# First graph of a fused hypergraph and expert kernel: load order, magnitudes, degrees and order of work rewritten

## The chip, the cores and the metric

The kernel runs on one core of a Trainium2 chip. The metric is the device time of one execution in microseconds. Three executions of the kernel before took 727.12, 729.49 and 731.59 us (median 729.49).

## The reference

For each of 16 graphs, x is 512 x 256 and adj is 512 x 512:

```python
def hypergraph_conv(x, adj, W, b):
    H = (adj != 0); w = adj.reshape(N, -1)[:, :C]         # w is the first row of adj
    Dn = 1 / (H @ w)                                      # 0 where the sum is 0
    Be = 1 / H.sum(axis=1)                                # one over the degree of each hyperedge
    return Dn * (H @ (Be * (H.T @ (x @ W.T)))) + b
x = x + [ln -> conv(W1, b1) -> relu -> layer_norm(gamma, beta) -> conv(W2, b2), + its input]
x = x + [ln -> router, top 2 of 4 experts, silu, mask, out_w, + its input, rms norm]
```

## The kernel before, in words

Matmul operands are split into two float16 halves (hi and lo), so each product is two or three matmuls. A weight is first scaled by a power of two from its largest magnitude. The scale therefore needs, before any half is made: the weight loaded, the magnitude of each partition (`setup_abs_*` on ScalarE, `setup_mag_*` on VectorE), a transpose to one row (`turn_mags`), its maximum (`largest`), a matmul that spreads it over the partitions (`spread_max`), and a chain of small VectorE operations (`setup_scale_a`, `_b`, `_c` for W1, for gamma times W2 called w2g, and for the experts, out_w and the router). `setup_hi` on ScalarE and `setup_lo` on VectorE then make the halves.

`steps` calls `body` per graph on each engine. Step 0 holds only the convolution of graph 0 (`conv=True, ffn=False`) and the set-up. Step g from 1 holds the convolution of graph g and the expert layer of graph f = g - 1; a tail follows. Nothing plans the order: each engine works through its own list in program order and waits on semaphores.

One convolution on TensorE is: A1 = H.T x (`first` lines L1453, L1454), D (L1466, the product with w), A2 (`a2_half`, L1421), A3 with W1 (L1310 to L1312), transposes of the normed h (`transposed_h`), V with w2g (`v_tile`), U and B3 (`incidence`). ScalarE takes each result out of PSUM as hi (`a1_part`, `hnt_part`, `v_part`), VectorE as lo. GpSimd turns variances into scale and bias (`root`) and adds x, b2 and the bias row to `xb` by three accumulating DMAs (`add_x`, `add_b2`, `add_v`), each behind the one before. `x1_half` adds B3 to `xb`; from x1 come statistics, roots, `x2_part`, the turned x2, its halves `xth` and `xtl`, router and experts.

In step 0 the DMA queue of SyncE issues wrow, x, beta, gamma, W2, adj, W1, b1, adj transposed, then the six loads of the expert part. `first_ht` makes the transposed incidence in four pieces, each summing its degree; for all later graphs `count_edges` on ScalarE counts degrees. In step 0, PE opens with `beta_w2`. The magnitudes use a buffer `absbuf`, written by ScalarE and reduced by VectorE.

Of the kernel before, what the change touches and what calls it, by code (L numbers as in the profile page):

```python
# [47 lines left out]
def build(nc, x, adj, adjt, wrow, w1t, b1, gamma, beta, w2t, b2, rw, rb, ew, eb, ow, ob, nw, out):  # L48
# [7 lines left out]
    with ExitStack() as ctx:  # L56
# [3 lines left out]
        def sem(name):  # L60
# [4 lines left out]
        A1_BANK, D_BANK, A2_BANK = (0, 3), 2, (4, 1)  # L65
# [25 lines left out]
        absbuf = sb("absbuf", [P, 2, 1024], F32)  # L91
# [11 lines left out]
        ident16 = sb("ident16", [P, P], F16)  # L103
        epsln, epsrms = sb("epsln", [P, CT], F32), sb("epsrms", [P, CT], F32)
# [67 lines left out]
        table_set, a_abs, b_abs, c_abs, a_hi, b_hi, c_hi = (  # L172
            sem(n) for n in ("table_set", "a_abs", "b_abs", "c_abs", "a_hi", "b_hi", "c_hi"))
# [3 lines left out]
        a_lo, b_lo, c_lo = (sem(n) for n in ("a_lo", "b_lo", "c_lo"))  # L177
        bw_rdy, vb_set = sem("bw_rdy"), sem("vb_set")
# [62 lines left out]
        def _(sp):  # L241
            sp.dma_start(wf[:, :, :], wrow).then_inc(wrow_in, 16)
            sp.dma_start(xin[:, :, :], x[0]).then_inc(x_in, 16)
            for dst, src in ((bet[:, :], beta), (gam[:, :], gamma),
                             (w2f[:, :, :], w2t.rearrange("(k p) f -> p k f", p=P))):
                sp.dma_start(dst, src).then_inc(b_in, 16)
            sp.dma_start(adjin[:, :, :], adj[0].rearrange("(t p) e -> p t e", p=P)).then_inc(adj_in, 16)
            for dst, src in ((w1f[:, :, :], w1t.rearrange("(k p) h -> p k h", p=P)),
                             (b1b[:, :], b1.to_broadcast([P, DH]))):
                sp.dma_start(dst, src).then_inc(a_in, 16)  # L250
            sp.dma_start(adjtin[:, :, :], adjt[0].rearrange("(t p) c -> p t c", p=P)).then_inc(adjt_in, 16)
# [9 lines left out]
            def body(sp, g, odd, conv, ffn, late, prep):  # L261
# [14 lines left out]
                if prep:  # L276
                    sp.wait_ge(ht_made, g + 4)
# [19 lines left out]
        def _(gp):  # L297
# [13 lines left out]
            gp.wait_ge(tables, 12)  # L311
# [6 lines left out]
            for i, part in enumerate((0, NE)):  # L318
                gp.wait_ge(tables, 15 + i)
# [81 lines left out]
            prep_x(0, again=False)  # L401

            def body(gp, g, odd, conv, ffn, late, prep):
# [19 lines left out]
                if conv:  # L423
                    if not ffn:
                        add_x(g)
# [1262 lines left out]
```

## Time and profile before

| | |
|---|---|
| runs | 727.12, 729.49, 731.59 us |
| profiled execution | 727.4 us, span 725.9 us |
| mean granted TensorE clock | 0.989 |
| PE busy | 685.4 us, 94% |
| DVE busy | 622.8 us, 86% |
| ACT busy | 528.7 us, 73% |
| POOL busy | 342.7 us, 47% |
| chain that ended last | PE 87%, DVE 5%, ACT 3% |

PE is TensorE's matmuls, DVE is VectorE, ACT is ScalarE, POOL is GpSimd, SPq is SyncE's queue. Times are from the start of the span. The span is 1.5 us shorter than that execution's own time, which in turn is 2.1 us under the median of the runs.

### The profile page before, as it was taken

The numbers are of one execution on the slowest core, as the hardware profiler recorded it, in microseconds if no ns is written. First come the engines' busy times: TensorE is split into PE (matmuls) and PEld (weight loads), VectorE is DVE, ScalarE is ACT, GpSimd is POOL, SyncE is SP. The second block draws the span as 40 slices with busy tenths as digits, with TensorE's granted clock in tenths as the row PEclk, the third lists the DMA queues.
The fourth block names the chain that finished last, engine by engine and source line by source line (L and its number), as shares of the span: only waits on it lengthen the run. The fifth ranks groups of instructions, "written<-read, shape, count | busy, mean of one in ns | idle before, by whom it ended". The sixth has DMA issues, their size and how long they took to land.

```text
span 725.9 us, 15857 instructions
## 1 busy us (share of the span) xinstructions
PE 685.4 (94%) x5197; PEld 475.7 (66%) x5197; DVE 622.8 (86%) x1544; ACT 528.7 (73%) x1091; POOL 342.7 (47%) x731
## 2 busy tenths in 40 slices
PE   3777999999999999999999999999999999999982
PEld 2464485866758586775858577685857668585672
DVE  3987799898989989898989989898998989898676
ACT  4567868688696868778686877869686786967563
POOL 4142625456373545646354554635355563634433
PEclk9999999999999999999999999999999999999997
DMA  8547449575665938566583947657394756537312
GB/s 284 190 77 242 92 106 235 93 236 117 210 141 136 230 63 256 112 212 134 153 203 61 274 99 227 120 173 173 83 260 90 236 111 197 121 77 184 59 30 59
DMA packets 42591, 111.72 MB, mean 154 GB/s; under 512 B 4161, under 2 KB 5313, under 8 KB 42561
## 3 DMA queue, kind: packets, MB, share of 16 engines
q0 software_dynamic: 13536, 41.42, 32.8%
q1 hardware_dynamic: 29024, 69.92, 27.4%
q8 instruction: 16, 0.26, 0.1%
q14 instruction: 15, 0.11, 0.0%
HBM read 69.91 MB, written 16.25 MB: 119 GB/s over the span
## 4 chain that ended last, share of the span: by engine, by line
PE 87%; DVE 5%; ACT 3%; DMA 1%; issue 1%; POOL 1%; SPq 0%; POOLq 0%; DVEq 0%; ACTq 0%
PE bank L1310 16%; PE bank L1312 16%; PE bank L1311 16%; PE bank L1395 7%; PE bank L1396 7%; PE bank L1421 7%; PE bank L1453 4%; PE bank L1454 4%; PE bank L1364 4%; PE bank L1357 2%; PE bank L1412 2%; DMA b1b<-b 1%; PE bank L1466 1%; PE bank L1345 0%; ACT x L591 0%
## 5 line engine op out<-in xcount | busy, mean ns | idle before, releaser
L1310 PE MATMUL bank<-xth,ewh 128*128 128x512 f16 (+1 forms) x272 | 100.4, 369 | 2.6 <-DVE ewl L827 2.6
L1311 PE MATMUL bank<-xtl,ewh 128*128 128x512 f16 (+1 forms) x272 | 100.3, 369 | 0.0
L1312 PE MATMUL bank<-xth,ewl 128*128 128x512 f16 (+1 forms) x272 | 100.3, 369 | 0.0
L536 ACT ACTIVATE silu<-bank,ebcol,ksc 128x512 f32<-128x512 f32 x120 | 89.7, 769 | 7.7 <-PE bank L1312 4.0
L399 POOL TENSOR_TENSOR comb<-comb,silu 128x1024 f32<-128x1024 f32 x30 | 74.3, 2478 | 0.6 <-DVE silu L904 0.6
L1310 PE MATMUL bank<-w2h,hnth 128*128 128x256 f16 x256 | 70.3, 275 | 0.1
L1311 PE MATMUL bank<-w2l,hnth 128*128 128x256 f16 x256 | 70.2, 274 | 0.0
L1312 PE MATMUL bank<-w2h,hntl 128*128 128x256 f16 x256 | 70.2, 274 | 0.0
L926 DVE SCALAR_TENSOR_TENSOR hntl<-bank,hnth 128x512 f16<-128x512 f32 x64 | 42.7, 687 | 26.8 <-ACT hnth L554 25.6
L1453 PE MATMUL bank<-xsh,h 128*128 128x256 f16 x256 | 59.0, 279 | 3.1 <-DVE xsl L809 2.4
L904 DVE TENSOR_TENSOR silu<-silu,bank 128x1024 f32<-128x1024 f32 x45 | 54.7, 1216 | 7.9 <-ACT silu L536 7.8
L384 POOL TENSOR_TENSOR yme<-yms,epsrms 128x4 f32<-128x4 f32 (+1 forms) x17 | 3.9, 228 | 119.0 <-ACT ysq L571 112.6
L1454 PE MATMUL bank<-xsl,h 128*128 128x256 f16 x256 | 58.9, 279 | 0.0
L1395 PE MATMUL bank<-vh,h 128*128 128x256 f16 x256 | 56.9, 273 | 1.5 <-DVE vl L931 1.5
L1396 PE MATMUL bank<-vl,h 128*128 128x256 f16 x256 | 56.9, 273 | 0.0
L549 ACT ACTIVATE hn<-r,hnb,hrs 128x512 f32<-128x512 f32 x64 | 52.0, 812 | 2.1 <-POOL hnb L331 2.1
L1310 PE MATMUL bank<-w1h,a2h 128*128 128x512 f16 x128 | 48.5, 379 | 0.8 <-DVE a2l L1092 0.8
L919 DVE BATCH_NORM_STATS2 hbn<-r 128x6 f32<-128x512 f32 x64 | 42.9, 671 | 6.9 <-ACT r L545 6.8
L1311 PE MATMUL bank<-w1l,a2h 128*128 128x512 f16 x128 | 48.5, 379 | 0.0
L1312 PE MATMUL bank<-w1h,a2l 128*128 128x512 f16 x128 | 48.5, 379 | 0.0
L915 DVE SCALAR_TENSOR_TENSOR z<-bank,dna,b1b 128x512 f32<-128x512 f32 x64 | 46.7, 748 | 1.6 <-PE bank L1312 0.2
L1312 PEld LDWEIGHTS bank<-xth,ewl 128*128 128x128 f16 x272 | 26.7, 98 | 29.2 <-issue 0.8
(273 smaller groups left out, 2072.7 us busy)
## 6 DMA issues: line engine op xcount, KB each, us to landing
adjin<-adj SPq DMA_DIRECT2D x16, 1024.0 KB, 5.4
adjtin<-adjt SPq DMA_DIRECT2D x16, 1024.0 KB, 7.9
xin<-x SPq DMA_DIRECT2D x16, 512.0 KB, 7.1
xb<-xn SPq DMA_DIRECT2D x16, 512.0 KB, 4.1
xb<-x POOLq DMA_DIRECT2D x16, 512.0 KB, 8.9
xb<-b POOLq DMA_DIRECT2D x16, 512.0 KB, 5.4
xb<-vadd POOLq DMA_DIRECT2D x16, 512.0 KB, 4.5
out<-x SPq DMA_DIRECT2D x15, 512.0 KB, 4.9
```

Of the source, the lines that this page charges most:

```text
L399: tt(comb[:, :, :], comb[:, :, :], silu[:, 2 * (e % 2):2 * (e % 2) + 2, :], ALU.add).then_inc(half_sum, 1)
L536: af(silu[:, i % 4, :], bank[E_BANK[i]][:, :], ACT.Silu, bias=ebcol[:, i:i + 1], scale=ksc[:, 2:3]).then_inc(silu_dn, 1)
L549: af(hn[:, t, :], r[:, t, :], ACT.Identity, bias=hnb[:, t:t + 1], scale=hrs[:, t:t + 1]).then_inc(hn_dn, 1)
L904: TT(src, src, m, ALU.mult).then_inc(comb_st, 1)
L1310: mm(outp, lh, rh, start=first, stop=False)
L1311: mm(outp, lh, rl, start=False, stop=False)
L1312: return mm(outp, ll, rh, start=False, stop=last)
L1395: mm(b, weights[:, k, P * e:P * e + P], hi[:, k, :], start=(k == 0), stop=False)
L1396: ins = mm(b, weights[:, k, P * e:P * e + P], lo[:, k, :], start=False, stop=(k == CT - 1))
L1421: ins = mm(bank[A2_BANK[d]][:, :], a[:, k, P * d:P * d + P], ht16[odd][:, k, :], start=(first and k == 0), stop=(last and k == CT - 1))
L1453: mm(b, h16[:, k, P * e:P * e + P], xsh[:, k, :], start=(k == 0), stop=False)
L1454: ins = mm(b, h16[:, k, P * e:P * e + P], xsl[:, k, :], start=False, stop=(k == CT - 1))
```

## The change

- SyncE issues adj, W1 and the transposed adj directly behind x; gamma, W2, beta and b1 follow.
- GpSimd multiplies W2 by gamma, where ScalarE did. It scales Dn in two pieces (`scale_dna`, `scale_dnb`), and forms the roots of the second graph's x (`prep_x(1)`) between `add_x` and `add_b2`.
- ScalarE makes x of the first graph in two halves (`first_x`) ahead of all weight work. A magnitude is the sum of the absolute values of a partition, from the ScalarE instruction's own accumulator (`sum_abs`); out_w and the router keep a maximum, on VectorE (`largest_abs`).
- TensorE counts degrees of graphs 0 and 1 (`count_products`, 16 products of one column); `first_ht` goes.
- TensorE runs 18 matmuls of zeros before the first product and 5 behind each of two transposes (`keep_busy`); `beta_w2` moves behind A3.
- In step 0, VectorE, ScalarE and TensorE take part of their work in another order; in step 1 the halves of the expert weights are made in another order, `ewh` at the end of step 0.

Cut, each line moved left by eight columns:

```diff
-    for dst, src in ((bet[:, :], beta), (gam[:, :], gamma),
-                     (w2f[:, :, :], w2t.rearrange("(k p) f -> p k f", p=P))):
+    sp.dma_start(adjin[:, :, :], adj[0].rearrange("(t p) e -> p t e", p=P)).then_inc(adj_in, 16)
+    sp.dma_start(w1f[:, :, :], w1t.rearrange("(k p) h -> p k h", p=P)).then_inc(a_in, 16)
+    sp.dma_start(adjtin[:, :, :], adjt[0].rearrange("(t p) c -> p t c", p=P)).then_inc(adjt_in, 16)
+    for dst, src in ((gam[:, :], gamma), (w2f[:, :, :], w2t.rearrange("(k p) f -> p k f", p=P)),
+                     (bet[:, :], beta), (b1b[:, :], b1.to_broadcast([P, DH]))):
         sp.dma_start(dst, src).then_inc(b_in, 16)
...
-    sp.dma_start(adjin[:, :, :], adj[0].rearrange("(t p) e -> p t e", p=P)).then_inc(adj_in, 16)
-    for dst, src in ((w1f[:, :, :], w1t.rearrange("(k p) h -> p k h", p=P)),
-                     (b1b[:, :], b1.to_broadcast([P, DH]))):
-        sp.dma_start(dst, src).then_inc(a_in, 16)
-    sp.dma_start(adjtin[:, :, :], adjt[0].rearrange("(t p) c -> p t c", p=P)).then_inc(adjt_in, 16)
...
-    def scale_dn(g):
+    def scale_dna(g):
         gp.wait_ge(d_step, 4 * g + 4)
         tt(dna[:, :], dn[:, :], ksc[:, 0:1].to_broadcast([P, CT]), ALU.mult).then_inc(dn_scaled, 1)
+    def scale_dnb(g):
         tt(dnb[:, :], dn[:, :], ksc[:, 1:2].to_broadcast([P, CT]), ALU.mult).then_inc(dn_scaled, 1)
...
+    gp.wait_ge(b_in, 64)
+    tt(w2g[:, :, :], w2f[:, :, :], gam[:, :].unsqueeze(2).to_broadcast([P, KH, D]), ALU.mult).then_inc(w2g_dn, 1)
...
-                gp.wait_ge(b_scale, 1)
-            scale_dn(g)
+                gp.wait_ge(a_scale, 1)
+            scale_dna(g)
+            if ffn:
+                scale_dnb(g)
...
             add_up(f, 1)
         if conv:
             if not ffn:
+                gp.wait_ge(b_scale, 1)
+                scale_dnb(g)
                 add_x(g)
+                prep_x(g + 1)
             add_b2(g)
         if ffn:
             add_up(f, 2)
         if conv:
-            if not ffn:
-                prep_x(g + 1)
             add_v(g)
...
+    def sum_abs(col, src):
+        n = src.shape[1] * src.shape[2]
+        return af(silu[:, :, :].rearrange("p k n -> p (k n)")[:, 0:n], src[:, :, :].rearrange("p k n -> p (k n)"),
+                  ACT.Abs, accum_out=mags[:, col:col + 1])
+    def first_x():
+        act.wait_ge(xrs_st, 4)
+        for j in range(2):
+            s = slice(CG * j, CG * j + CG)
+            for t in range(CG * j, CG * j + CG):
+                af(xn[:, t, :], xin[:, t, :], ACT.Identity, bias=xnb[:, t:t + 1],
+                   scale=xrs[:, t:t + 1]).then_inc(xn_dn, 1)
+            act.wait_ge(xn_dn, CG * j + CG)
+            af(xsh[:, s, :], xn[:, s, :], ACT.Copy, scale=XS).then_inc(xs_hi if j else x0_hi, 1)
...
+    first_x()
+    act.wait_ge(tables, 16)
+    act.wait_ge(a_in, 16)
+    sum_abs(W1, w1f).then_inc(a_mag, 1)
...
-        if conv and ffn and not late:
-            setup_hi(c_scale, ((ewf, ewh, EX),), c_hi)
...
-                setup_abs_ew()
-                setup_hi(b_scale, ((w2g, w2h, W2),), b_hi)
+                act.wait_ge(a_mag, 1)
+                act.wait_ge(w2g_dn, 1)
+                sum_abs(W2, w2g).then_inc(b_mag, 1)
...
-        if conv:
-            if ffn:
-                norm_h(act, g, 0)
+        if conv and ffn:
+            norm_h(act, g, 0)
             relu(act, g, 3)
         if ffn:
             expert(act, f, 3)
         if conv:
             norm_h(act, g, 1)
+        if conv and not ffn:
+            hnt_part(act, g, 0)
+            setup_hi(b_scale, ((w2g, w2h, W2),), b_hi)
+            relu(act, g, 3)
+            hnt_part(act, g, 1)
         if ffn:
             expert(act, f, 4)
         if conv:
-            if not ffn:
-                hnt_part(act, g, 0)
             norm_h(act, g, 2)
             if not ffn:
-                setup_abs_c()
-                bias_rows(act, g)
+                act.wait_ge(b_mag, 1)
+                act.wait_ge(c_in, 16 * 6)
+                sum_abs(EX, ewf).then_inc(ew_sum, 1)
         if ffn:
             expert(act, f, 5)
         if conv:
             if ffn:
                 hnt_part(act, g, 0)
-            else:
-                hnt_part(act, g, 1)
             norm_h(act, g, 3)
         if conv:
             if ffn:
...
             expert(act, f, 7)
         if conv:
             hnt_part(act, g, 2)
+            if not ffn:
+                v_part(act, g, 0)
             hnt_part(act, g, 3)
-            v_part(act, g, 0)
+            if ffn:
+                v_part(act, g, 0)
+            else:
+                bias_rows(act, g)
         if ffn:
             ct_part(act, f, 0)
             ct_part(act, f, 1)
...
         if conv:
             for e in range(CT):
                 if e % CG == 0:
+                    if not ffn:
+                        prep_x(g + 1, range(e, e + CG))
                     act.wait_ge(u_rdy, 2 * g + e // CG + 1)
                 af(uh[:, e, :], bank[U_BANK[e // CG]][:, D * (e % CG):D * (e % CG) + D], ACT.Copy,
                    scale=be[odd][:, e:e + 1]).then_inc(u_hi, 1)
         if conv and not ffn:
-            prep_x(g + 1, range(CT))
             prep_x_hi(g + 1)
-            setup_hi(c_scale, ((rwf, rwh, RW), (owf, owh, OW)), c_hi)
+            setup_hi(c_scale, ((rwf, rwh, RW), (ewf, ewh, EX), (owf, owh, OW)), c_hi)
         if ffn and prep:
             squares(act, f, 0)
             squares(act, f, 1)
-        if prep:
-            count_edges(act, g, 1 - odd)
+        if prep and ffn:
+            count_edges(act, g, 1 - odd, late)
...
+    def largest_abs(col, src):
+        return v.reduce_max(mags[:, col:col + 1], src, X, apply_absolute_value=True)
+    def first_lo(j):
+        s = slice(CG * j, CG * j + CG)
+        dve.wait_ge(xs_hi if j else x0_hi, 1)
+        STT(xsl[:, s, :], xn[:, s, :], XS, xsh[:, s, :], ALU.mult, ALU.subtract).then_inc(xs_lo if j else x0_lo, 1)
...
+    def degrees(g, odd, counted_by_pe):
+        if counted_by_pe:
+            dve.wait_ge(deg_rdy, g + 1)
+        else:
+            dve.wait_ge(deg_dn, 4 * g - 4)
+        TS(dmax[:, :], bank[DEG_BANK][:, DEG] if counted_by_pe else deg[:, :], 1.0, None, ALU.max).then_inc(be_max, 1)
         dve.wait_ge(be_max, g + 1)
         v.reciprocal(be[odd][:, :], dmax[:, :]).then_inc(be_dn, 1)
+    prep_h(0, again=False)
+    first_lo(0)
+    degrees(0, 0, True)
+    first_lo(1)
...
-                first_ht()
-                degrees(0, 0)
+                prep_ht(0, 0)
                 largest(a_turn, slice(W1, W1 + 1), 0, a_top)
-                setup_mag_b()
         if conv and ffn and not late:
-            setup_lo(c_hi, 2, ((rwf, rwh, rwl, RW), (owf, owh, owl, OW)), c_lo)
+            setup_lo(c_hi, 1, ((rwf, rwh, rwl, RW),), c_lo)
         if conv:
             a1_part(g, odd, 0)
         if late:
...
             if not ffn:
                 setup_scale_a()
             a1_part(g, odd, 1)
+            if not ffn:
+                d_vector(g)
...
         if conv and not ffn:
-            largest(b_turn, slice(W2, W2 + 1), 1, b_top)
             setup_lo(a_hi, 1, ((w1f, w1h, w1l, W1),), a_lo)
         if prep and ffn:
             prep_x_stats(g + 1, (0, 1))
+        if conv and ffn and not late:
+            setup_lo(c_hi, 2, ((ewf, ewh, ewl, EX),), c_lo)
...
+            setup_lo(c_hi, 3, ((owf, owh, owl, OW),), c_lo)
...
-                setup_scale_b()
-                d_vector(g)
-            dve.wait_ge(dn_scaled, 2 * g + 1)
+                dve.wait_ge(b_in, 64)
+            dve.wait_ge(dn_scaled, (2 * g if ffn else g) + 1)
             z_part(g, 0)
         if conv:
             z_part(g, 1)
...
                 v.memset(spare[:, :], 0.0)
                 h_aggr(g, 0)
             z_part(g, 2)
+            if not ffn:
+                largest(b_turn, slice(W2, W2 + 1), 1, b_top)
             if ffn:
                 h_aggr(g, 0)
             h_stats(g, 1)
             dve.wait_ge(hbn_dn, 4 * g + 2)
+            if not ffn:
+                v.memset(spare[:, :], 0.0)
+                h_aggr(g, 1)
+                h_stats(g, 2)
+                dve.wait_ge(hbn_dn, 4 * g + 3)
+                v.memset(spare[:, :], 0.0)
+                h_aggr(g, 2)
+                setup_scale_b()
             z_part(g, 3)
-            h_aggr(g, 1)
-            if not ffn:
+            if ffn:
+                h_aggr(g, 1)
+                h_stats(g, 2)
+        if ffn:
+            combine(f, 0)
+        if conv:
+            if ffn:
+                dve.wait_ge(hbn_dn, 4 * g + 3)
+                v.memset(spare[:, :], 0.0)
+                h_aggr(g, 2)
+            else:
+                hnt_part(g, 0)
                 setup_lo(b_hi, 1, ((w2g, w2h, w2l, W2),), b_lo)
-            h_stats(g, 2)
-        if ffn:
-            combine(f, 0)
-        if conv:
-            dve.wait_ge(hbn_dn, 4 * g + 3)
-            v.memset(spare[:, :], 0.0)
-            h_aggr(g, 2)
             h_stats(g, 3)
             dve.wait_ge(hbn_dn, 4 * g + 4)
             v.memset(spare[:, :], 0.0)
             h_aggr(g, 3)
-            if not ffn:
-                hnt_part(g, 0)
-                setup_mag_ew()
         if ffn:
             combine(f, 1)
         if conv and ffn:
...
         if conv:
             hnt_part(g, 1)
             if not ffn:
+                setup_mag_ow()
                 setup_mag_c()
         if ffn:
             combine(f, 3)
         if conv:
             hnt_part(g, 2)
-        if conv:
-            hnt_part(g, 3)
-        if ffn:
-            combine_sum(f)
-        if conv:
-            if not ffn:
-                largest(c_turn, slice(EX, RW + 1), 2, c_top)
-        if ffn:
-            ct_part(f, 0)
-        if conv:
-            v_part(g, 0)
             if not ffn:
                 prep_x_stats(g + 1)
                 prep_x_aggr(g + 1)
+        if conv:
+            hnt_part(g, 3)
+        if ffn:
+            combine_sum(f)
+        if ffn:
+            ct_part(f, 0)
+        if conv:
+            v_part(g, 0)
+            if not ffn:
+                largest(c_turn, slice(EX, RW + 1), 2, c_top)
...
+    def keep_busy(n):
+        for _ in range(n):
+            mm(bank[7][:, :], m16[:, 0, :], m16[:, :, :].rearrange("p t c -> p (t c)"), start=True, stop=True)
+    def count_products():
+        for e in range(CT):
+            for k in range(CT):
+                ins = mm(bank[DEG_BANK][:, DEG][:, e:e + 1], h16[:, k, P * e:P * e + P], one16[:, :],
+                         start=(k == 0), stop=(k == CT - 1))
+        ins.then_inc(deg_rdy, 1)
+    def first_aggregation():
+        def part(e, ks):
+            b = bank[A1_BANK[e // CG]][:, D * (e % CG):D * (e % CG) + D]
+            for k in ks:
+                mm(b, h16[:, k, P * e:P * e + P], xsh[:, k, :], start=(k == 0), stop=False)
+                ins = mm(b, h16[:, k, P * e:P * e + P], xsl[:, k, :], start=False, stop=(k == CT - 1))
+            return ins
+        pe.wait_ge(x0_lo, 1)
+        part(0, (0, 1))
+        part(CG, (0, 1))
+        pe.wait_ge(xs_lo, 1)
+        part(0, (2, 3))
+        part(1, range(CT)).then_inc(a1_rdy, 1)
+        part(CG, (2, 3))
+        turn_mags(a_mag, 1, slice(W1, W1 + 1), 0, a_turn)
+        part(CG + 1, range(CT)).then_inc(a1_rdy, 1)
...
-            if not ffn:
-                beta_w2()
             pe.wait_ge(h_made, g + 1)
             if late:
                 pe.wait_ge(y_dn, 2 * (g - 1))
-            pe.wait_ge(xs_lo, g + 1)
-            for e in range(CT):
-                if ffn and e == 0:
+            else:
+                count_products()
+            if not ffn:
+                first_aggregation()
...
+                if not ffn and t == 1:
+                    turn_mags(b_mag, 1, slice(W2, W2 + 1), 1, b_turn)
...
+            if not ffn:
+                spread_max(b_top, 1, 1, b_max)
+                beta_w2()
             transposed_h(g, 0)
+            if not ffn:
+                keep_busy(5)
             transposed_h(g, 1)
+            if not ffn:
+                keep_busy(5)
         if ffn:
             expert_half(f, 6)
             mask_rows(f, 3, g, conv)
...
         if conv:
             v_tile(g, 0)
             transposed_h(g, 2)
-            transposed_h(g, 3)
+            if ffn:
+                transposed_h(g, 3)
             v_tile(g, 1)
+            if not ffn:
+                transposed_h(g, 3)
             v_tile(g, 2)
         if conv:
             if not ffn:
-                turn_mags(c_mag, slice(EX, RW + 1), 2, c_turn)
+                turn_mags(c_mag, 1, slice(EX, RW + 1), 2, c_turn)
             v_tile(g, 3)
             if not ffn:
                 spread_max(c_top, 4, 2, c_max)
...
         last_out(0)
         last_out(1)
-    pe.wait_ge(tables, 17)
+    pe.wait_ge(tables, 12)
+    keep_busy(18)
```

## Rows read from the trace of the kernel before

**Rows 1.** Busy time in stretches: stretch, length, busy (count) of PE, PEld, DVE, ACT, POOL, clock, DMA, GB/s.

```profile
0.00:57.00 57.00, 37.60 (x233) 25.04 (x233) 39.51 (x110) 31.94 (x55) 18.25 (x59) 0.97 0.61 183
57.00:84.00 27.00, 22.46 (x144) 12.14 (x145) 22.17 (x67) 20.18 (x41) 9.65 (x28) 0.94 0.71 205
84.00:109.00 25.00, 25.00 (x207) 20.28 (x206) 21.11 (x42) 17.46 (x40) 11.37 (x21) 1.00 0.35 82
```

**Rows 2.** PE in order of time: start, duration, operation, count, [idle before, releaser].

```profile
14.29 0.37 PE L1453 MATMUL bank<-xsh,h 128*128 128x256 f16 x1 [2.41 <-DVE xsl L809]
...
22.32 1.04 PE L1421 MATMUL bank<-ht_even,a1h 128*128 128x512 f16 x4
...
27.02 0.38 PE L1310 MATMUL bank<-w1h,a2h 128*128 128x512 f16 x1 [0.77 <-DVE a2l L1092]
...
38.57 0.37 PE L1310 MATMUL bank<-w2h,hnth 128*128 128x256 f16 x1
...
57.45 0.27 PE L1453 MATMUL bank<-xsh,h 128*128 128x256 f16 x1 [0.65 <-issue]
...
60.94 0.54 PE L1466 MATMUL bank<-wcur,ht_odd 128*128 128x4 bf16 x16
...
70.88 0.39 PE L1310 MATMUL bank<-xth,ewh 128*128 128x512 f16 x1 [2.56 <-DVE ewl L827]
...
71.61 0.63 PE L1310 MATMUL bank<-xth,ewh 128*128 128x512 f16 x1
```

**Rows 3.** SyncE's queue in order of time: start and length of two issues.

```profile
3.39 0.51 SPq L247 DMA_DIRECT2D adjin<-adj  x1
...
5.00 0.46 SPq L251 DMA_DIRECT2D adjtin<-adjt  x1
```

**Rows 4.** DVE in order of time, columns as for PE.

```profile
11.78 1.23 DVE L779 TENSOR_SCALAR h<-adjin 128x2048 f16<-128x2048 f32 x1 [4.81 <-DMA adjin<-adj]
12.92 1.22 DVE L809 SCALAR_TENSOR_TENSOR xsl<-xn,xsh 128x1024 f16<-128x1024 f32 x1
...
17.29 0.69 DVE L784 TENSOR_SCALAR_CACHE_REDUCE ht_even<-adjtin 128x512 f16<-128x512 f32 x1 [0.44 <-DMA adjtin<-adjt]
...
34.07 1.25 DVE L827 SCALAR_TENSOR_TENSOR w2l<-w2g,wsc,w2h 128x1024 f16<-128x1024 f32 x1
...
57.27 0.87 DVE L1023 SCALAR_TENSOR_TENSOR x<-bank,dnb,xb 128x256 f32<-128x256 f32 x2
...
68.48 2.34 DVE L827 SCALAR_TENSOR_TENSOR ewl<-ewf,wsc,ewh 128x2048 f16<-128x2048 f32 x1
```

**Rows 5.** ACT in order of time.

```profile
9.62 2.06 ACT L470 ACTIVATE xn<-xin,xnb,xrs 128x256 f32<-128x256 f32 x4
11.71 1.06 ACT L477 ACTIVATE xsh<-xn 128x1024 f16<-128x1024 f32 x1
...
64.12 1.99 ACT L528 ACTIVATE ewh<-ewf,wsc 128x2048 f16<-128x2048 f32 x1
```

**Rows 6.** POOL in order of time.

```profile
8.61 0.20 POOL L331 TENSOR_TENSOR xnb<-xnm,xrs 128x4 f32<-128x4 f32 x1
...
34.23 1.14 POOL L326 TENSOR_TENSOR hve<-hmv,epsln 128x1 f32<-128x1 f32 x1 [0.88 <-DVE hmv L922]
...
36.37 0.19 POOL L326 TENSOR_TENSOR hve<-hmv,epsln 128x1 f32<-128x1 f32 x1
...
51.00 1.23 POOL L374 DMA_DIRECT2D xb<-vadd  x1
...
86.27 2.36 POOL L399 TENSOR_TENSOR comb<-comb,silu 128x1024 f32<-128x1024 f32 x1
```

**Rows 7.** DMA issues by tensor, 36 to 60 us: count, size, us from issue to landing.

```profile
xb<-x POOLq DMA_DIRECT2D x1, 512.0 KB, 5.8
xb<-b POOLq DMA_DIRECT2D x1, 512.0 KB, 5.4
xb<-vadd POOLq DMA_DIRECT2D x1, 512.0 KB, 4.8
```

More of the change, by code:

```diff
@@ L779, in prep_h @@
                 TS(h16[:, :, :], adjin[:, :, :], 0.0, None, ALU.not_equal).then_inc(h_made, 1)
-            def first_ht():
-                dve.wait_ge(adjt_in, 16)
-                for t in range(CT):
-                    TS(ht16[0][:, t, :], adjtin[:, t, :], 0.0, None, ALU.not_equal, ALU.add,
-                       accum_out=deg[:, t:t + 1]).then_inc(ht_made, 1)
-                dve.wait_ge(ht_made, CT)
             def prep_ht(g, odd):
@@ L1049, in body @@
                 if conv and ffn:
-                    degrees(g, odd)
+                    degrees(g, odd, not late)
                 if ffn:
@@ L1084, in body @@
                 if conv and ffn and not late:
-                    setup_lo(c_hi, 3, ((ewf, ewh, ewl, EX),), c_lo)
+                    setup_lo(c_hi, 3, ((owf, owh, owl, OW),), c_lo)
                 if conv and ffn:
@@ L1126, in body @@
                 if conv:
-                    dve.wait_ge(hbn_dn, 4 * g + 3)
-                    v.memset(spare[:, :], 0.0)
-                    h_aggr(g, 2)
+                    if ffn:
[4 more added lines that the diff above has]
+                        hnt_part(g, 0)
+                        setup_lo(b_hi, 1, ((w2g, w2h, w2l, W2),), b_lo)
                     h_stats(g, 3)
@@ L1379, in out_product @@
                 pe.wait_ge(ct_lo, 2 * f + j + 1)
+                if isinstance(f, int) and f == 0:
+                    pe.wait_ge(c_lo, 3)
                 for t in range(CG * j, CG * j + CG):
@@ L1444, in body @@
                         pe.wait_ge(y_dn, 2 * (g - 1))
-                    pe.wait_ge(xs_lo, g + 1)
-                    for e in range(CT):
-                        if ffn and e == 0:
+                    else:
+                        count_products()
+                    if not ffn:
+                        first_aggregation()
+                    else:
+                        pe.wait_ge(xs_lo, g + 1)
+                    for e in range(CT if ffn else 0):
+                        if e == 0:
                             pe.wait_ge(hnt_lo, 4 * g)
-                        if ffn and e == CG:
+                        if e == CG:
                             pe.wait_ge(u_lo, 4 * (g - 1) + 2)
@@ L1456, in body @@
                             ins.then_inc(a1_rdy, 1)
-                        if not ffn and e == 0:
-                            turn_mags(a_mag, slice(W1, W1 + 1), 0, a_turn)
-                    pe.wait_ge(ht_made, g + 4)
+                    pe.wait_ge(ht_made, g + 1)
                     pe.wait_ge(w_cur, g + 1)
@@ L1478, in body @@
                     a2_half(g, odd, 1, ffn)
[L1479 to L1480 removed]
                 if ffn:
                     if not late:
[L1484 removed]
+                        pe.wait_ge(c_lo, 1)
                     for t in range(CT):
```

106 lines of the change are left out of this document (33 added, 73 removed).

## The prediction

> **What bounds the kernel now.** I first read busy time in stretches [rows 1]. From 84 us on PE is busy in all of every stretch: the first is shown, and the ten that follow up to 680 us read the same, at clock 1.00. Before that, PE stands for 57.00 - 37.60 = 19.4 us in the first 57 and for 4.5 us up to 84. So nothing in the steady part is touched by this change, and its worth is how much earlier PE enters the full stretch. Next I read PE in order of time for the start of each stage and what ended the wait before it [rows 2]: A1 of graph 0 at 14.29, A2 at 22.32, A3 at 27.02, V at 38.57, A1 of graph 1 at 57.45, the first expert product at 70.88. I then followed the releaser of each on its own engine [rows 4 to 6]. Two facts bound the start. The two adjacency loads, issued at 3.39 and 5.00 [rows 3], release VectorE at 11.78 and 17.29 [rows 4]; and x, whose bias is ready on GpSimd at 8.81 [rows 6], stands behind w2g on ScalarE until 9.62 [rows 5].
>
> **A1 of graph 0.** adj is issued about 1.4 us earlier (each issue takes some 0.5 [rows 3]) and 512 KB of W2 no longer lie in front of it. I put its landing at 8.4; the ends are 7.7 and 11.8, the latter if order changes nothing. h costs 1.23 [rows 4], so it is made by 9.6 (13.0). ScalarE starts x at 8.85: half of 2.06 and half of 1.06 [rows 5] give the first hi half at 10.5, the second at 12.1. VectorE's half of 1.22 [rows 4], taken as 0.7 for its fixed part, gives 11.3 and, with the two small degree operations between, 12.9. PE counts degrees from 9.7 in 0.54, the price of the 16 narrow products of D [rows 2]. Thirty-two A1 products take 60.94 - 57.45 = 3.49, or 0.109 each [rows 2]. Eight are done before 12.9, 24 after: A1 ends at 15.6. The 18 products of zeros lie in idle time: at the slow spacing of 0.43 each (a duration of 0.63 against 0.38 [rows 2]) they end at 3.0 + 7.7 = 10.7, still before the first half of x is ready.
>
> **A2.** The transposed adj is now the fourth load, 0.75 MB behind fewer bytes and issued 2 us earlier. I put it at 12.5 to 13 (ends 11.5 and 17.3). `prep_ht` is one operation at the price of h, 1.23, where `first_ht` took four of 0.69 [rows 4]: done by 14.3, before A1 ends. W1's magnitude is the accumulator of an absolute-value pass, 1.06 by the xsh row [rows 5], so the transposed magnitude is there at 15.1 and its maximum at 15.6. D 0.54, one small product: A2 starts at 16.6, 5.7 earlier than 22.32.
>
> **A3.** Before, A2 to A3 is 27.02 - 22.32 = 4.7. The scale chain loses a copy (0.2), but `d_vector`, five operations of 0.2, now stands ahead of W1's lo half, of which I let 0.2 reach the path. A3 starts at 16.6 + 4.9 = 21.5, 5.5 earlier.
>
> **V.** Before, 38.57 - 27.02 = 11.55. The w2g magnitude now hangs on GpSimd: one product of 1024 elements, 2.36 by the comb row [rows 6], behind all four small loads (about 15), so w2g at 17.5, long before ScalarE asks at 21.2. The second scale chain moves behind the third statistics, then hi 1.15 and lo 1.25 [rows 4] stand in front of V as before. My sum on VectorE is z of tile 3 at 30.8, w2h at 31.9, w2l at 33.2. V starts at 33.3, 5.3 earlier. beta times W2, twice five zero products and the transposes end at 32.7 beside it.
>
> **V to A1 of graph 1.** Before, 57.45 - 38.57 = 18.9. Off: V's first tile at the fast spacing, 12 products at 0.1 = 1.2, as PE no longer stands in front of it; the 2048-element reduce. On: statistics of graph 1's x, 1.9, ahead of the last lo half of h, and 0.54 for counting. B3 then ends at 51.3 and A1 begins at 51.8, 5.6 earlier.
>
> **x1 of graph 0.** This hangs on three DMAs behind each other. Their prices are 5.8, 5.4 and 4.8 [rows 7]. Before: the last is issued at 51.00 [rows 6] and lands at 55.8; `x1_half` starts at 57.27 behind VectorE's own queue [rows 4]. After: `add_x` at 35.7 behind the last root, landed 41.5; but `add_b2` is queued behind `prep_x(1)`, which waits for statistics ready at 39.9 and takes 2.0, so it goes out at 42.0, lands at 47.5, and the last goes out at 47.7 and lands at 52.5. VectorE is free at 51.1. So the wait for the DMA takes 1.4 us and `x1_half` starts at 52.5, 4.8 earlier.
>
> **First expert product.** Before, 70.88 - 57.27 = 13.6. Removed ahead of it: ewh 1.99 on ScalarE in front of xth [rows 5], and owl (0.75) on VectorE. ewl, 2.34 [rows 4], stays in front, but now beside ScalarE's work on x2. Counting by ScalarE goes too, though the roots hide it. ewl ends at 62.1, both xtl at 63.4: experts at 63.7, 7.2 earlier. PE's last wait is then short, so the slow stretch that begins there may vanish: eight products at 0.43 instead of 0.216 cost 1.7 [rows 2], which would make 8.9.
>
> That 1.7 is not mine to count in full. VectorE still owes owl, `d_vector` and the a2 lo halves, ready at 67.5 against 73.2 (5.7 earlier), then the routing. The mask copy on ScalarE comes 6.3 earlier, and the normed h that PE transposes about 6: it had near 1 us of slack, so PE may come 7.2 to 7.5 earlier, whatever its clock. I take **7.2**. The span becomes 718.7, the profiled execution 720.2; against the median of the runs, which lies 2.1 above the profiled one, 729.5 - 7.2 = **722.3**.
>
> **Two rules weighed.** In the trace, a small root beside w2l took 1.14 where it otherwise takes 0.19 [rows 4, 6], so the two engines can hold each other up. The Trainium skill (SBUF — State Buffer, section SBUF: two separate sides) says that VectorE, in some forms, and GpSimd share a port pair under an exclusive lock for a whole instruction; the row agrees. By the lone row, the sum stands at 722.3; by the rule, the 2.36 of w2g could hold VectorE, which is rival 3. For the clock, PE ran at the lower of its two levels, 1.2 instead of 2.4 GHz, after its wait of 2.56 [rows 2]. The Trainium skill (TensorE: Matmul & The Clock Gate, section What's actually happening) says that the throttled state is the default and activity releases it; no row here shows whether products of zeros count.
>
> **Rivals.**
> 1. Everything keeps pace and the fast clock holds: 8.9 earlier, 720.6. For: all waits after 84 us are zero. Against: VectorE is only 6 earlier. Chance 0.14.
> 2. The loads interleave, so order hardly matters and the transposed adj comes at 15 to 17. A2 starts at 19 instead of 16.6, 2.4 lost: 724.7. For: the two landings of before are 5.5 apart for 1.75 MB, near what all loads share. Chance 0.12.
> 3. w2g on GpSimd lands on `prep_ht` or the scale chain and holds VectorE for its whole 2.36 [rows 6]: 724.7. By the page on SBUF this is what happens if the two meet. Against: they meet only if the small loads land between 12 and 17 while VectorE needs that port. Chance 0.12.
> 4. Zeros don't raise the clock: A1's last 24 products and V's first tile cost 0.1 more each, 3.6 in all, partly hidden: 725. Chance 0.09.
> 5. The DMA chain takes longer than one by one before, 1 us on each: `x1_half` 3 later, 725.3. Chance 0.09.
> 6. **Slower.** `add_b2` now waits in GpSimd's queue for graph 1's statistics, and those wait in VectorE's queue for ScalarE's sum over the expert weights, which waits for the last of fifteen loads. Each us of delay of that sum past 36.8 moves x1. The gain is gone when it is 7.2 late; at 14.5 late the time is 737. Against: before, these loads were in by about 22. Chance 0.04.
>
> The forecast itself has 0.40. A measurement of this kernel tells about 1%, 7.3 us, from no change, so 7.2 earlier lies on that border: I give half of the forecast's 0.40, all of rival 1 and 0.04 from the others to faster, 0.38; 0.04 and a little of what I do not see to slower, 0.05; the rest, 0.57, within 1%. The range takes rivals 1 to 5 with about 2.5 us for the runs' own spread, which also covers two of them in part together: 718 to 728.
>
> **What would show it.** In the changed trace: h at or before 9.6 and the transposed one before 14.5 (rival 2: later); A1 products 0.11 apart (rival 4: 0.21); the w2g product on GpSimd with no VectorE operation stretched beside it (rival 3); A2, A3 and V near 16.6, 21.5 and 33.3; `x1_half` released by the DMA near 52.5 (rivals 5 and 6: later); experts near 63.7 and their spacing; and a short PE wait for z, the mask or h in the 12 us behind. The forecast is wrong if PE has waits beyond 84 us that it had not, or if a moved operation delays another's queue by over 2 us.

## The result and the profile after

The changed kernel took **760.86 us** (median of four runs, 758.83 to 761.55), the kernel before 728.81 beside it: a ratio of 1.0432, 95% interval 1.0407 to 1.0458. The forecast was 722.3 and no range of mine reached 760. The profiled execution took 761.47 us with a span of 759.9, against 727.4.

I began where the prediction had: busy time in stretches, columns as in [rows 1].

```profile
0.00:57.00 57.00, 45.16 (x325) 29.84 (x325) 36.28 (x108) 31.33 (x53) 21.06 (x64) 0.97 0.69 207
57.00:84.00 27.00, 24.50 (x152) 12.44 (x153) 23.41 (x65) 21.55 (x41) 13.49 (x36) 1.00 0.56 157
84.00:109.00 25.00, 25.00 (x233) 20.23 (x232) 23.37 (x59) 16.34 (x41) 9.84 (x18) 1.00 0.62 176
...
200.00:250.00 50.00, 44.62 (x324) 30.16 (x323) 38.20 (x95) 32.93 (x68) 21.43 (x45) 0.93 0.62 147
300.00:350.00 50.00, 44.75 (x323) 30.36 (x322) 37.80 (x94) 32.55 (x68) 21.68 (x45) 0.93 0.54 137
```

Up to 109 us the changed kernel is ahead. The loss lies in the steady part, where the trace of before had PE busy in all of every stretch at clock 1.00: in the two stretches shown last, PE stands about 5.3 us in 50 and the granted clock is 0.93, while PE is busy in all of the stretch between them. The waits of VectorE and of PE, from 60 us on (total, times, longest), say at what:

```profile
DVE x L1011 <- issue: 33.4, 5, 6.8
```

```profile
PE bank L1505 <- DVE x L1011: 23.5, 5, 4.8
```

"Issue" is idle time with nothing to wait for. It occurs five times, and the kernel's loop over graphs 3 to 14 (`Fori(3, N - 2, 2)`) has six iterations, so five returns. VectorE in order of time around the first return, with PE behind it:

```profile
222.32 1.22 DVE L782 TENSOR_SCALAR h<-adjin 128x2048 f16<-128x2048 f32 x1
230.33 0.88 DVE L1011 SCALAR_TENSOR_TENSOR x<-bank,dnb,xb 128x256 f32<-128x256 f32 x2 [6.79 <-issue]
...
233.06 0.57 PE L1505 MATMUL bank<-wcur,ht_odd 128*128 128x4 bf16 x16 [4.79 <-DVE x L1011]
234.21 1.89 PE L1459 MATMUL bank<-ht_odd,a1h 128*128 128x512 f16 x4 [0.59 <-ACT a1h L573]
```

The h product is the last operation of the body, x the first of it. `add_v` had been issued at 214.9 and landed 4.6 us later, so x1's data were there. Four products that take 1.03 elsewhere take 1.89 behind the stall. The granted clock stands at its lower level (1.2 of 2.4 GHz) from 231.1 to 238.0 us, so it falls while PE still stands and works against PE only from 233.06 on (columns as above):

```profile
231.00:233.00 2.00, 0.00 (x0) 0.00 (x0) 1.94 (x9) 0.00 (x0) 0.69 (x3) 0.53 0.00 0
233.00:238.00 5.00, 4.36 (x28) 2.42 (x29) 4.86 (x16) 4.18 (x9) 3.01 (x7) 0.50 0.77 252
```

Now the branch itself (sequencer rows of the line of the loop: count, ns, first and last start), in the changed kernel and, below, in one shown later whose loop runs well:

```profile
L232 DVEq COMPARE_BRANCH  x6: 55/63/63, 221.9 to 680.7; - x6
```

```profile
L233 DVEq COMPARE_BRANCH  x6: 50/56/67, 221.8 to 640.2; - x6
```

One iteration takes (680.7 - 221.9) / 5 = 91.8 us against 83.7. Five times 8.1 is **40.4 us**: the 34.1 by which the profiled execution is longer, and what the front gained. The last clue is section 3 of the page, the packets that load instructions (count, MB), before and after:

```profile
q14 instruction: 15, 0.11, 0.0%
```

```profile
q14 instruction: 39, 0.32, 0.1%
```

From 222 to 640 us the changed kernel has 25 packets of 8192 bytes, five for each return (222.4, 222.9, 228.3, 230.8 and 268.2 us, and so on); the kernel before has none between 223 and 650 us. (The page of before counts one small packet in its first microsecond, so the totals differ by 24.) A loop that has run once is being read again from memory.

### The profile page after: what moved, and what is told of

The parts are those of the page before. It is cut to its first block, busy times and chain, and to the rows that moved or that the text cites. A ratio compares the mean times of both kernels' runs of the same rounds, so it can differ in the third digit from the quotient of the medians.

```text
span 759.9 us, 15946 instructions
## 1 busy us (share of the span) xinstructions
PE 702.6 (92%) x5257; PEld 482.3 (63%) x5257; DVE 617.1 (81%) x1533; ACT 524.2 (69%) x1081; POOL 345.0 (45%) x733
## 4 chain that ended last, share of the span: by engine, by line
PE 78%; DVE 8%; issue 6%; ACT 4%; DMA 2%; POOL 1%; DVEq 0%; POOLq 0%; ACTq 0%; SPq 0%
PE bank L1316 15%; PE bank L1318 15%; PE bank L1317 15%; PE bank L1459 8%; PE bank L1403 6%; PE bank L1404 6%; PE bank L1370 3%; PE bank L1420 2%; PE bank L1495 2%; PE bank L1494 2%; PE bank L1363 2%; DVE x L1011 1%; DMA xb<-vadd 1%; DVE h L782 1%; DMA xb<-b 1%
## 5 line engine op out<-in xcount | busy, mean ns | idle before, releaser
L914 DVE SCALAR_TENSOR_TENSOR hntl<-bank,hnth 128x512 f16<-128x512 f32 x64 | 42.7, 686 | 26.4 <-ACT hnth L550 25.5
L1011 DVE SCALAR_TENSOR_TENSOR x<-bank,dnb,xb 128x256 f32<-128x256 f32 x64 | 27.5, 472 | 39.5 <-issue 33.4
L1494 PE MATMUL bank<-xsh,h 128*128 128x256 f16 x240 | 53.2, 273 | 0.0
L1495 PE MATMUL bank<-xsl,h 128*128 128x256 f16 x240 | 53.2, 273 | 0.0
```

Of the source, the lines that this page charges most:

```text
L1494: mm(b, h16[:, k, P * e:P * e + P], xsh[:, k, :], start=(k == 0), stop=False)
L1495: ins = mm(b, h16[:, k, P * e:P * e + P], xsl[:, k, :], start=False, stop=(k == CT - 1))
```

## The experiments

**Theory:** VectorE's loop (261 instructions, 260 before: that many rows stand in the trace from one branch to the next) lies at a place in the code where it no longer stays in VectorE's instruction store. **Rivals:** the three accumulating DMAs behind each other hold x; or 261 instructions are one too many anywhere. The first experiments change nothing but how many VectorE instructions stand ahead of the loop. Where one time is given for a kernel, it was executed once.

**1. Ten, three, one idle instructions ahead.** In the changed kernel, n = 10, 3 or 1:

```diff
+            for i in range(n):
+                v.memset(pads[:, i:i + 1], 0.0)
             prep_x_stats(0)
```

> The changed kernel with ten stores of one column each ahead of VectorE's first work, in the time in which it waits for x anyway (about 0.6 us of 5). They do nothing but move all of VectorE's later code by ten instructions. Theory (placement): the loop body of 261 VectorE instructions lies, in the changed kernel, where it no longer stays in VectorE's instruction store, and is read again from memory at each of the five returns to its start; ten instructions further on it is resident again. Then the five idle stretches of 6.8 us ahead of the first x go, the 8 KB instruction packets between 230 and 650 us go, TensorE's clock stays at full level there, and the time is 720 to 724 us (760.9 less 5 x 6.8 less 5 x 0.8 from the halved clock, near the forecast of 722.3). Rival (DMA chain): x waits for the three accumulating DMAs of GpSimd, which the change stretched; ten stores change nothing in that, and the time stays at 759 to 762 us. Rival (one instruction more in the loop, 261 for 260, is itself too many): the stores change nothing either, 759 to 762 us.

> As the run before, with three stores in place of ten: where the edge is. Counted in blocks of 128 instructions (the 8 KB packets), the loop of the changed kernel would begin in the last few of a block and so touch four blocks, and one that begins a few instructions later touches three. Placement theory: either side is possible, 720 to 724 us if three instructions are enough to reach the next block, 760 us if not; anything between the two speaks against the theory. Both rivals: 759 to 762 us.

> The changed kernel with one store ahead of VectorE's work. It says only how near the edge the changed kernel stands: 720 to 724 us if it is the last bad place, 759 to 762 us if not. A time between them would speak against a threshold.

Measured: n = 10 took 720.1, 720.1 and 725.7 us, and one run of 818.4, with a granted clock of 0.844 where the others have 0.984 to 0.992, that nothing here explains; the ratio of the other three to before is 0.989 (0.984 to 0.995). n = 3 took 721.6. n = 1 took 750.9. **Three stores of 0.06 us are worth 39 us**, and both rivals fall: the transfers and the 261 instructions were the same in all three. That each of these kernels has one tile more, `pads`, is not the cause either: the kernels of experiment 3 with spacers left out show both the loss and its absence with no tile added. The page of n = 3 is back at 15 packets:

```profile
q14 instruction: 15, 0.11, 0.1%
```

I had written that a time between the two speaks against a threshold; 750.9 looks like one. The waits of n = 1 show that it isn't between: still five stalls, 5.1 us in the mean where the changed kernel has 6.7.

```profile
DVE x L1014 <- issue: 25.6, 5, 6.1
```

**2. The kernel before, put there.** With 118 or 246 stores added, or with `spacer()` in place of the one-column stores that stand as spacers, which stores nothing in its first ten calls:

```diff
-                v.memset(spare[:, :], 0.0)
+                spacer()
```

> The kernel before, with 118 stores of one column on VectorE (62 ahead of its first work, 56 while it waits for the first adj), so that its loop begins at the place in a block of 128 that it has in the changed kernel (ten before that of the kernel before). Nothing else is changed. Placement theory with blocks of 128: stalls of about 6.8 us at each return to the loop's start, packets of 8 KB in the steady part, and 729 plus about 35 to 40 plus up to 2 for the stores in the first graph: 762 to 772 us. Placement theory with larger blocks (256): the place differs, and the time is 729 to 732 us. DMA-chain rival: the loads and the order are those of the kernel before, so 729 to 732 us. Rival (261 for 260 instructions): 729 to 732 us.

> The kernel before, less ten of the one-column stores that stand as spacers on VectorE ahead of bn_aggr in the first three graphs (0.06 us each); the loop itself keeps its 260 instructions. Its loop now begins at the very position, counted from VectorE's first instruction, at which that of the changed kernel begins. Placement theory: this kernel, which holds nothing of the change, shows the whole loss: five stalls of about 6.8 us ahead of the first x at the returns, the clock at half level for 6.8 us behind each, 729 + 5 x 8 = 766 to 772 us; if one instruction fewer in the loop is just enough for it to fit, 729 us. Rival (DMA chain of the changed kernel) and rival (261 against 260 instructions): 727 to 732 us.

> The kernel before with 246 stores on VectorE (126 ahead of x, 120 ahead of the first adj; 62 and 56 of them took 1.8 and 1.0 us and cost nothing in the run before). Its loop begins 256 places behind that of the kernel before less ten. Placement theory with blocks of 256 instructions: the loss returns, 766 to 772 us plus up to 3 for the stores. If only the distance from the start of the program counts, and not the place in a block of 256: 729 to 733 us.

Measured: 731.0, 729.1 (0.9988, 0.9966 to 1.0011) and 731.4 us. **Three misses**: none showed the loss. Either the theory was wrong for the kernel before, or my count was. It was the count. `first_ht` sums while it converts [rows 4], and the trace shows that as two instructions, four times; the program that I had counted holds one:

```profile
L784 DVE TENSOR_SCALAR_CACHE_REDUCE ht_even<-adjtin x4: 681/682/686, 17.3 to 19.1; 128x512 f16<-128x512 f32 x4
L784 DVE DVE_READ_ACCUMULATOR ht_even<-adjtin x4: 83/83/84, 17.9 to 19.7; 128x1 f32 x4
```

So the loop of before starts 14 behind that of the changed kernel, not 10, and all three stood four instructions off the place (126 ahead of a boundary, where 2 or 130 was wanted). Where the place is, the changed kernel's own trace says. After the return, two sequencer instructions of the new iteration pass by 225.4 us, and the third waits until 230.2; in the kernel with one store, one passes (223.2) and the second waits until 227.4. Rows of the second and third instruction of the changed kernel (its first stands at 225.3):

```profile
L1006 DVEq FUSED_REGOPS  x1: 46/46/46, 225.4 to 225.4; - x1
...
L1008 DVEq EVENT_SEMAPHORE  x1: 21/21/21, 230.2 to 230.2; - x1
```

The loop begins **two instructions ahead of a boundary**. How many instructions lie between boundaries, the three misses say: their programs differ only by 128 stores each (10 less, 118 more, 246 more), and their pages count 14, 15 and 16 instruction packets. So a packet of 8192 bytes holds 128 instructions, 64 bytes each. 2 + 128 + 128 + 3 = 261 touches four such blocks; from five or more ahead, or behind the boundary, it touches three.

**3. Four tests of that rule**, each able to break it: the kernel before with 14 spacers less and with 114 stores more, the changed kernel with two and with three spacers less. A fifth kernel, with eight spacers less, ran beside those of experiment 2, when I still counted in blocks of 256; it is no test between the two block sizes.

> The kernel before, less fourteen one-column spacer stores. Ten were not enough to put its loop where the changed kernel has it: four of its VectorE operations with an accumulator execute as two instructions each (TENSOR_SCALAR_CACHE_REDUCE and DVE_READ_ACCUMULATOR, four of each in its trace), which the count of the program did not hold. The changed kernel waits behind exactly two instructions after each return, and with one store ahead of it behind one: its loop begins two instructions ahead of a boundary, the 8 KB packets are 128 instructions of 64 bytes, and 261 instructions that begin 2, 1 (or 4, 3) ahead of a boundary touch four blocks, at every other place three. Fourteen fewer put the 260 of the kernel before also two ahead: placement theory 766 to 772 us, two instructions let through at each return and then a wait. Rivals (accumulating DMAs of the change; 261 against 260 instructions): 727 to 732 us.

> The kernel before with 114 one-column stores on VectorE (62 ahead of x, 52 ahead of the first adj): two ahead of the next boundary of 128. Placement theory with blocks of 128: 766 to 772 us. With blocks of 256: 729 to 733 us, and 242 stores would be needed.

> The changed kernel less two spacers: its loop begins four ahead of a boundary and ends with its branch as the first instruction of the fourth block. Theory of four blocks: the last bad place, 752 to 762 us, and VectorE waits behind four instructions after each return instead of two. Theory of a wider or narrower bad stretch: 720 to 724 us.

> The changed kernel less three spacers: its loop begins five ahead of a boundary and its branch is the last instruction of the third block. Theory of four blocks: 720 to 724 us; if the chip reads on ahead before the branch is taken, 752 to 762 us, and the rule is one place wider.

> The changed kernel less eight such spacers in its first three graphs: its loop begins eight instructions earlier. With 18 of 256 places shown or held good (from three behind to ten behind) and one bad, the placement theory with a loop of 261 and its branch in a store of 512 (two blocks of 256) has a bad stretch of six to eight places, all within seven ahead of the changed kernel's: 720 to 724 us. If the bad stretch is wider (a store that holds less than 512), 759 to 762 us.

Measured: 769.3 (ratio 1.055, 1.048 to 1.062), 769.9, 757.6, 720.0 and 721.6 us. All five lie in the ranges written for them, and as the rule of four blocks has them. Blocks of 256 fall: 14 less and 114 more are 128 apart and both bad. The kernel before, less fourteen stores that do nothing, is 40 us slower, with the rows of the changed kernel:

```profile
DVE x L1030 <- issue: 33.2, 5, 6.9
```

```profile
L230 DVEq COMPARE_BRANCH  x6: 55/63/72, 228.2 to 688.0; - x6
L1025 DVEq FUSED_REGOPS  x1: 46/46/46, 231.8 to 231.8; - x1
L1027 DVEq EVENT_SEMAPHORE  x1: 21/21/21, 236.2 to 236.2; - x1
```

With two spacers less, four instructions pass, as written, and the fifth is the first that waits:

```profile
L1013 DVEq FUSED_REGOPS  x1: 46/46/46, 224.2 to 224.2; - x1
L1016 DVEq ALU_OP  x1: 40/40/40, 224.4 to 224.4; - x1
L1018 DVE SCALAR_TENSOR_TENSOR x<-bank,dnb,xb x2: 473/478/483, 228.5 to 228.9; 128x256 f32<-128x256 f32 x2
```

| kernel | loop | starts, to the next boundary | blocks | us |
|---|---|---|---|---|
| changed | 261 | 2 | 4 | 760.9 |
| changed, 1 store | 261 | 1 | 4 | 750.9 |
| changed, 2 less | 261 | 4 | 4 | 757.6 |
| changed, 3 less; 8 less | 261 | 5; 10 | 3 | 720.0; 721.6 |
| changed, 3 stores; 10 stores | 261 | 127; 120 | 3 | 721.6; 720.1 |
| before | 260 | 116 | 3 | 728.8 |
| before, 10 less; 118; 246 stores | 260 | 126 | 3 | 729.1; 731.0; 731.4 |
| before, 14 less; 114 stores | 260 | 2 | 4 | 769.3; 769.9 |

The Trainium skill (Runtime: NRT & Kernel Launch, section Instruction fetch mechanics) says that a taken branch whose target has left the store of 512 instructions forces a fetch before execution goes on; the traces agree: VectorE stands up to 6.8 us in the changed kernel, in two parts. The branch is at 221.9, the first instruction of the new iteration at 225.3 and the third, behind the boundary, at 230.2. It gives blocks of 256 instructions, and there the measurement differs: VectorE's packets hold 128.

**4. What the first graph brought**, at the good place with ten stores (720.1 us). Load order back; and `keep_busy` made empty:

```diff
             def keep_busy(n):
+                return
```

> The changed kernel with its ten stores (good place, 720.1 us in its profiled execution), SyncE's loads back in the order of before: beta, gamma and W2 ahead of adj, W1, b1 and the transposed adj. VectorE's code is the same, so the place of its loop is too. What the load order brought: adj is issued about 1.4 us later and shares the engines with W2, so h starts 2.3 to 2.7 us later (11.4 to 11.8 us) and the first graph with it: 722 to 723 us. Rival (the DMA chain of the bias sets x1 in any case, and starts from the weights): 720 us.

> The changed kernel with its ten stores, without the 28 products of zeros. What they brought: without them the clock is at half when the first product starts, and A1, D, A2 and A3 of the first graph run in part at half speed: 3 to 6 us of products before the clock rises, of which the chain of small operations between A3 and V hides little: 722 to 725 us. Rival (the zeros hide behind waits for VectorE and ScalarE, as my rival of zeros that do not help had it): 720 to 721 us.

Measured: 724.0 us (five runs, 723.1 to 724.2) and 721.6 (four, 721.5 to 724.9). The load order is worth 2.4 to 3.9 us of the 9 (from the 721.6 and the 720.1 of the good place), and 724.0 lies above the 722 to 723 that I wrote; h starts at 11.47 with the old order, where it started at 8.4:

```profile
11.47 1.23 DVE L783 TENSOR_SCALAR h<-adjin 128x2048 f16<-128x2048 f32 x1 [4.63 <-DMA adjin<-adj]
```

The zeros are worth little, and the 722 to 725 that I wrote missed: three of the four runs without them lie at 721.6, at the end of the 720.0 to 721.6 of the good place, so 0 to 1.5 us stays unresolved. The first products do run slowly without them, 20 of them 0.2 apart:

```profile
12.17 0.40 PE L1444 MATMUL bank<-xsh,h 128*128 128x256 f16 x1 [1.91 <-DVE xsl L842]
12.36 0.42 PE L1445 MATMUL bank<-xsl,h 128*128 128x256 f16 x1
```

The parts that moved work between engines were not undone one by one; the 3 to 6 us left of the 9 are theirs together, which is a difference and not a measurement of any.

**5. The three additions earlier.** In both kernels x1 of graph 0 stands at the end of three accumulating DMAs.

```diff
                     for t in range(CT):
+                        if not ffn and t == 2:
+                            add_x(g)
                         root(hstat, ...)
...
                         scale_dnb(g)
-                        add_x(g)
+                        add_b2(g)
                         prep_x(g + 1)
-                    add_b2(g)
+                    else:
+                        add_b2(g)
```

> The changed kernel with its ten stores and GpSimd's program in the first graph in another order: x is added to xb between the second and the third root of h (28.4 us, in place of 34.4), b2 behind the scaling of Dn (34.4, in place of 40.2, behind the roots of the second graph's x), so the bias rows follow at about 40.5 in place of 46.2 us. The three additions are what x1 waits for (3.9 us of VectorE, 2.3 us of TensorE ahead of the second D). Theory: x1 starts at 49 us, as soon as VectorE is free, D at 53.3 instead of 55.6, and the time falls by 2.3 us: 717 to 719 us, if the transfers take their 5.4 to 6.6 us. Rival (the 2.3 us come back at the halves of the expert weights, 2.3 us on VectorE ahead of the experts): 720 us.

Measured: **715.8 us** (six runs, 714.8 to 717.4; ratio to before 0.9815, 0.9787 to 0.9843). This is below both kernels, and below the 717 to 719 that I wrote. x, D of graph 1 and the first expert product with ten stores alone:

```profile
52.86 0.88 DVE L1014 SCALAR_TENSOR_TENSOR x<-bank,dnb,xb 128x256 f32<-128x256 f32 x2 [3.88 <-DMA xb<-vadd]
...
55.59 0.54 PE L1508 MATMUL bank<-wcur,ht_odd 128*128 128x4 bf16 x16 [2.26 <-DVE x L1014]
...
63.58 0.38 PE L1319 MATMUL bank<-xth,ewh 128*128 128x512 f16 x1
```

and with the additions early:

```profile
48.96 0.87 DVE L1017 SCALAR_TENSOR_TENSOR x<-bank,dnb,xb 128x256 f32<-128x256 f32 x2
...
53.36 0.54 PE L1511 MATMUL bank<-wcur,ht_odd 128*128 128x4 bf16 x16
...
59.75 0.38 PE L1322 MATMUL bank<-xth,ewh 128*128 128x512 f16 x1
```

x and D start where I put them. The gain between the two profiled executions was 3.9 us and not the 2.3 that I wrote, because I had read it from PE's wait for D alone. VectorE had 3.9 us of idle time, and VectorE's own queue, not D, set the first expert product: ewl, then xtl, which begins at 62.03 with ten stores alone and at 58.20 here. The rival had named that very work as the one that eats the gain; it was the one that passed it on whole.

## Why the prediction was wrong

The sentence that failed is in its first paragraph: "**nothing in the steady part is touched by this change**, and its worth is how much earlier PE enters the full stretch." The instructions and data of the steady part are nearly untouched. Its place in VectorE's code is not: the front lost 14 executed VectorE instructions (two for each of four `first_ht` pieces among them) and the loop gained one. At a good place the loop ran as in [rows 1], at this one each return costs 8.1 us. PE stands for 26.4 us between 200 and 650 us, 5.3 for each return (4.7 for x, 0.6 for a1h on ScalarE); the other 2.8 is the lower clock, by difference. From D to the first router product PE takes 7.3 us at the first return, and 4.7 in the kernel with three stores. My rival for the slower side had its mechanism in GpSimd's queue and ended at 737, and x1 at 54.6 us shows that it did not happen; no rival looked at the code's size. What did stand in the text is the sign by which it would show: "PE has waits beyond 84 us that it had not".

The rest of the working, against the changed kernel's trace and the same kernel with ten stores:

| step | predicted | changed | with ten stores |
|---|---|---|---|
| h begins | 8.4 | 9.1 | 8.4 |
| transposed adj converted, begins | 12.5 to 13 | 13.2 | 12.5 |
| A2 begins | 16.6 | 17.9 | 16.1 |
| A3 begins | 21.5 | 22.7 | 20.9 |
| V begins | 33.3 | 34.0 | 32.2 |
| A1 of graph 1 begins | 51.8 | 51.5 | 49.7 |
| x1 begins | 52.5 | 54.6 | 52.9 |
| first expert product | 63.7 | 65.3 | 63.6 |
| time | 722.3 | 760.9 | 720.1 to 725.7 |

The parts of the forecast, one by one:

- **Loads.** Right within 0.7 us. Rival 2 (they interleave) falls: the transposed adj is there at 13.2.
- **A1.** In the changed kernel's profiled execution PE stood 2.1 us ahead of the first product, and 16 A1 products ran 0.21 apart. That costs 1.6 us, where A2 was 1.3 later than I said:

```profile
12.84 0.40 PE L1440 MATMUL bank<-xsh,h 128*128 128x256 f16 x1 [0.59 <-DVE xsl L839]
13.03 0.42 PE L1441 MATMUL bank<-xsl,h 128*128 128x256 f16 x1
```

 With ten stores they ran 0.11 apart. The eight products ahead of these 16, behind the zeros, ran 0.11 apart in both kernels, and 0.2 apart without zeros. So rival 4's mechanism falls, but the zeros do not always reach far enough, and its price was half right: 1.6 us in one execution, nothing in another.
- **A3.** My terms were 4.7, less 0.2 and plus 0.2, and I added 4.9, a slip of 0.2; A2 to A3 took 4.8 in both kernels.
- **w2g on GpSimd.** Rival 3 falls. It ran at 15.45 for 1.89, less than my 2.36, behind `prep_ht` (13.18 for 1.23), and nothing on the path waited for it. VectorE's a1l at 16.93 took 0.85, in part beside it, no more than the next one alone (0.88), so no hold-up shows here:

```profile
15.45 1.89 POOL L406 TENSOR_TENSOR w2g<-w2f,gam 128x1024 f32<-128x1024 f32 x1 [3.48 <-DMA b1b<-b]
```

- **x1.** The mechanism was right, that the DMA chain takes over from VectorE's queue. The last transfer took 6.3 us for my 4.8 [rows 7], which is most of the 2.1 us on that row; rival 5, in part. VectorE waited 3.94 instead of 1.4:

```profile
54.60 0.88 DVE L1011 SCALAR_TENSOR_TENSOR x<-bank,dnb,xb 128x256 f32<-128x256 f32 x2 [3.94 <-DMA xb<-vadd]
```

- **Experts.** 63.6 at the good place for 63.7. The 7.2 us that I had for the front are 7.3 between the profiled executions at 720.1 and 727.4. The front was sized well, and it is the part that mattered less. In part that is luck: V to A1 of graph 1 took 17.5 us for my 18.5 and x1 to the experts 10.7 for my 11.2, and these make up for the DMA.
- **Rival 1.** The first expert products ran at the fast spacing (65.33, 65.97) and, at the good place, PE has no wait from 84 to 650 us, as it asked. Its 8.9 us can't be told from my 7.2: the medians 728.8 and 720.1 lie 8.7 apart, the profiled executions 7.3.

## What to carry to other kernels

When a change adds or removes instructions ahead of a loop, the place of that loop is part of the change. Ask for each engine how long its loop is and in how many blocks it can lie (only VectorE's was moved here). By the rule above, one of 257 instructions or fewer never touches four blocks of 128, and one of 261 does at 4 places of 128. Before crediting or blaming an edit, look in the new trace for idle time with no releaser at the loop's return and for a raised count of instruction packets, and if they are there, time the edit again with a few idle instructions in front. And count from the executed trace: one operation of the program can be two instructions.

## What the runs showed of the hardware

- A VectorE loop of 260 or 261 instructions that touches four blocks of 128 instructions is read again at every return, with five packets of 8 KB; one that touches three is not. This held in all 13 kernels in which the place was moved or read, with five bad ones. Why four blocks (512 instructions) do not stay is not shown; that a fifth block, fetched ahead, pushes out the first would fit the five packets, but no run separates it.
- An instruction packet of VectorE is 8192 bytes and holds 128 instructions: 128 more stores ahead of the loop add one packet (14, 15, 16).
- A return at a bad place holds VectorE 4.6 to 6.9 us. It matters how the instructions lie: with one ahead of the boundary the stalls were 4.6 to 6.1 us, the lower clock lasted half as long at three of the five returns (a granted clock of 0.93 over 25 us, where the changed kernel has 0.86), and the loss was 10 us less in all. Why they are shorter is open.
- A stall of 4.8 us on TensorE costs about 2.8 more through its clock: it stands at the lower level for 6.8 us, of which 1.9 lie in the stall itself at the first return, and the four products behind it take 1.89 us in place of 1.03.
- A sum taken from VectorE's accumulator executes as two instructions (TENSOR_SCALAR_CACHE_REDUCE and DVE_READ_ACCUMULATOR).
- A series of one-column stores on VectorE costs less than the 0.06 us that one takes: 61 in a row took 1.75 us, or 0.03 each.
